# Cross attention turned in 32x32 blocks by VectorE and exchanged through DRAM

## The reference, cut to what matters

```python
q = (hidden_states @ Wq.T).reshape(bsz, q_len, H, HD).transpose(0, 2, 1, 3)
k = (cross_attention_states @ Wk.T).reshape(bsz, kv_len, KVH, HD).transpose(0, 2, 1, 3)
v = (cross_attention_states @ Wv.T).reshape(bsz, kv_len, KVH, HD).transpose(0, 2, 1, 3)
q = _rmsnorm(q, q_norm_w)
k = jnp.repeat(k, GROUPS, axis=1)
v = jnp.repeat(v, GROUPS, axis=1)
k = _rmsnorm(k, k_norm_w)
scores = jnp.einsum('bhqd,bhkd->bhqk', q, k) * scale
scores = scores + attention_mask[:, :, :, :kv_len]
probs = jax.nn.softmax(scores.astype(jnp.float32), axis=-1).astype(q.dtype)
out = jnp.einsum('bhqk,bhkd->bhqd', probs, v)
return out @ Wo.T
```

## Time and profile before

| | |
|---|---|
| Median of 3 runs | 789.96 us (789.69 to 791.82) |
| Profiled execution | 791.35 us |
| Span, first to last instruction | 789.6 us |
| Mean granted TensorE clock | 0.998 of 2.4 GHz |
| TensorE busy | 773.5 us (98%) |
| TensorE weight loads | 635.0 us (80%) |
| VectorE, ScalarE, POOL busy | 559.5 (71%), 414.7 (53%), 365.8 us (46%) |
| Moved by DMA | 34.63 MB |

### The profile page before, as it was taken

One profiled execution on the slowest core, in us unless ns is written; L12 is line 12 of the kernel. 1 busy time (PEld: TensorE's weight loads), 2 busy tenths in 40 slices (PEclk: granted clock), 3 DMA queues, 4 the chain that ended last, 5 costly groups with the idle time before them and its releaser, 6 DMA issues.

```text
span 789.6 us, 13246 instructions
## 1 busy us (share of the span) xinstructions
PE 773.5 (98%) x4260; PEld 635.0 (80%) x4260; DVE 559.5 (71%) x1235; ACT 414.7 (53%) x1158; POOL 365.8 (46%) x429
## 2 busy tenths in 40 slices
PE   8899999989999999999999999999999999999998
PEld 5555665778888888888888888888888888788776
DVE  5888886667766766777777776676677777667874
ACT  5566654565456545654655555555555654355421
POOL 1668856564246324632553364336433533254532
PEclk9999999999999999999999999999999999999999
DMA  8311012021003100300031012002100201000011
GB/s 295 129 41 41 15 50 98 1 94 29 14 1 107 28 1 1 108 28 1 3 107 27 1 32 87 18 1 73 49 14 1 81 1 54 1 15 1 1 40 68
DMA packets 17124, 34.63 MB, mean 44 GB/s; under 512 B 2336, under 2 KB 2592, under 8 KB 16800
## 3 DMA queue, kind: packets, MB, share of 16 engines
q1 hardware_dynamic: 17056, 33.78, 13.5%
HBM read 31.67 MB, written 2.10 MB: 43 GB/s over the span
## 4 chain that ended last, share of the span: by engine, by line
PE 77%; DVE 8%; POOL 7%; issue 5%; ACT 1%; DMA 1%; SPq 0%; POOLq 0%; DVEq 0%; ACTq 0%
PE pair L862 18%; PE pair L863 18%; PE pair L864 18%; PE pair L964 4%; PE pair L977 3%; PE pair L1026 3%; PE pair L902 3%; POOL qkr L526 2%; PE pair L876 2%; POOL probn L518 2%; PE pair L966 1%; POOL wo_lo L512 1%; DVE xres L1325 1%; DVE score L1342 1%; PE pair L919 1%
## 5 line engine op out<-in xcount | busy, mean ns | idle before, releaser
L518 POOL TENSOR_TENSOR probn<-prob,erec 128x512 f32<-128x512 f32 x64 | 66.8, 1044 | 169.5 <-DVE erec L1357 169.5
L1381 DVE TENSOR_TENSOR qkn<-pair,qkr 128x640 f32<-128x640 f32 x64 | 52.8, 824 | 91.6 <-POOL qkr L526 91.6
L1362 DVE TENSOR_REDUCE qkss<-qksq 128x5 f32<-128x640 f32 x64 | 52.6, 821 | 84.4 <-ACT qksq L720 84.4
L713 ACT ACTIVATE prob<-score,nmax 128x128 f32<-128x128 f32 x256 | 99.6, 393 | 21.0 <-DVE nmax L1344 19.2
L702 ACT ACTIVATE oT_hi<-pair 128x512 fp32r<-128x512 f32 x64 | 38.1, 595 | 136.2 <-PE pair L864 136.2
L862 PE MATMUL pair<-wq_hi,nT_hi 128*128 128x512 f32 x256 | 106.6, 416 | 0.0
L862 PE MATMUL pair<-wo_hi,oT_hi 128*128 128x512 f32 x256 | 100.9, 394 | 2.8 <-issue 2.8
L864 PE MATMUL pair<-wq_hi,nT_lo 128*128 128x512 f32 x256 | 101.0, 394 | 0.0
L863 PE MATMUL pair<-wq_lo,nT_hi 128*128 128x512 f32 x256 | 100.9, 394 | 0.0
L863 PE MATMUL pair<-wo_lo,oT_hi 128*128 128x512 f32 x256 | 100.4, 392 | 0.0
L864 PE MATMUL pair<-wo_hi,oT_lo 128*128 128x512 f32 x256 | 99.8, 390 | 0.0
(11 more groups left out here) (178 smaller groups left out, 1985.0 us busy)
## 6 DMA issues: line engine op xcount, KB each, us to landing
wq_raw<-in_wq SPq DMA_DIRECT2D x32, 256.0 KB, 3.1
wo_raw<-in_wo SPq DMA_DIRECT2D x32, 256.0 KB, 2.9
wkv_raw<-in_wkv SPq DMA_DIRECT2D x8, 512.0 KB, 4.8
ctxn<-in_ctx_n SPq DMA_DIRECT2D x8, 256.0 KB, 3.6
ctxt<-in_ctx_t SPq DMA_DIRECT2D x8, 256.0 KB, 2.7
out<-wkv_raw SPq DMA_DIRECT2D x8, 256.0 KB, 2.0
xres<-in_x SPq DMA_DIRECT2D x1, 1280.0 KB, 8.3
wbase<-in_wbase SPq DMA_DIRECT2D x1, 1024.0 KB, 7.5
```

Of the source, the lines that this page charges most:

```text
L518: pool.tensor_tensor(probn[:], prob[:], erec[:].unsqueeze(2).broadcast_to([P, HG, P]), ALU.mult).then_inc(normed, 1)
L713: t = act.activation(prob[:, h, :], score[:, h, :], ACT.Exp, bias=nmax[:, h:h + 1], accum_out=esum[:, h:h + 1])
L1362: dve.tensor_reduce(qkss[:], qksq[:], AX.X, ALU.add).then_inc(qk_ss, 1)
L1381: dve.tensor_tensor(qkn[:], qk_bank, qkr[:].unsqueeze(2).broadcast_to([P, HG + 1, P]), ALU.mult).then_inc(qk_nat, 1)
```

## The change

Queries, keys and probabilities are no longer turned by TensorE. VectorE's transpose turns each 32x32 block of the tile where it lies (`turn_qk`, `turn_probs` on VectorE); then the blocks must change places between the four quarters of the partitions. SP does this through DRAM (`write_blocks`): four writes, one for each 32 partitions, in runs of 640 bytes (queries and keys) or 512 bytes (probabilities), then one read with 128 rows of 2560 or 2048 bytes. DRAM has two such places for each kind. The turned queries lie as four blocks of 32 rows of all four heads, so the scores of block i hold rows 32 i to 32 i + 31 of the four heads; mask, maxima, sums and probabilities follow that order.

The scores are four plain fp32 matmuls of 128 columns; the high and low parts of queries and keys are gone, and `scale_keys` on ScalarE writes the scaled keys once. The mask is loaded ready in the new order, into the place of four of the `dft` matrices, and added in one VectorE instruction. The normalised probabilities are written in place. The freed PSUM banks give the scores one bank, the projections two pairs in turn from unit 3 on (`buf`).

Every `slot` has a new order. On TensorE: probabilities times values of n - 3, projections of n + 2, scores of n, output projection of n - 3; the way from scores to values is one unit longer. In the last slots `feed_forward` stands ahead of `turn_batch`. The output weights are split at unit 3 of a group instead of 1. SP's loop runs over the units: it writes and reads the blocks, and the weight loads stand at fixed units behind them.

The diff, cut to its core:

```diff
+    WKV_AT, WO_AT = 0, 3
+    WQ_AT = {1: (0,), 2: (1,), 4: (2,), 5: (3,)}
...
+        def buf(n):
+
+            return 1 + (n % 2 if n >= 3 else 0)
...
+                def write_blocks(n, tile, dram, turned, read, done):
+
+                    sp.wait_ge(turned, n + 1)
+                    if n >= 2:
+                        sp.wait_ge(read[n % 2], landed(n - 2))
+                    q = P // BL
+                    for i in range(BL):
+                        sp.dma_start(dram[n % 2][:, :, i, :].rearrange("j z r -> z j r"),
+                                     tile[i * q:(i + 1) * q, :].rearrange("z (j r) -> z j r", j=BL)).then_inc(
+                                         done[n % 2], 16)
...
+                def read_qk(n):
+                    sp.wait_ge(qk_out[n % 2], BL * landed(n))
+                    need(sp, s_done, n - 1)
+                    sp.dma_start(qkT[n % 2][:].rearrange("p i h y -> p (i h y)"),
+                                 qk_dram[n % 2].rearrange("j z i r -> (j z) (i r)")).then_inc(qk_in[n % 2], 16)
+
+                def read_probs(n):
+                    sp.wait_ge(p_out[n % 2], BL * landed(n))
+                    need(sp, p_h, n)
+                    need(sp, p_l, n)
+                    sp.dma_start(pTf[:], p_dram[n % 2].rearrange("j z h r -> (j z) (h r)")).then_inc(p_in[n % 2], 16)
...
+                for n in range(-1, N + 1):
+                    g, b = n // B, n % B
+                    if on(n + 1):
+                        write_qk(n + 1)
+                    if n < 2 and on(n + 1):
+                        read_qk(n + 1)
+                    if on(n - 1):
+                        write_probs(n - 1)
+                    if n >= 2 and on(n + 1):
+                        read_qk(n + 1)
+                    if on(n - 1):
+                        read_probs(n - 1)
...
                 def scores(n):
...
-                    for h in range(HG):
-                        w = slice(h * P, (h + 1) * P)
-                        pe.matmul(s_bank[:, h, :, :].rearrange("p i t -> p (i t)"), qT_hi[:, w],
-                                  kT[:].rearrange("p i t -> p (i t)"), start=True, stop=True, skip_group_check=True)
-                        t = pe.matmul(s_bank[:, h, 0, :], qT_lo[:, w], kT[:, 0, :], start=False, stop=True,
+                    for i in range(BL):
+                        t = pe.matmul(s_bank[:, i, :], queries(n, i), kT[:], start=True, stop=True,
                                       skip_group_check=True)
...
                 def slot(n):
-                    late = n % B == 2
-                    if on(n):
-                        scores(n)
-                    if on(n - 1):
-                        turn_probs(n - 1)
+                    if on(n - 3):
+                        probs_v(n - 3)
...
+                    if on(n + 2):
+                        project_qkv(n + 2)
+                    if batch(n, FEED) is not None:
+                        feed_forward(batch(n, FEED))
+                    if batch(n, TURN) is not None:
+                        turn_batch(batch(n, TURN))
+                    if on(n):
+                        scores(n)
...
+                    if on(n - 3):
+                        project_out(n - 3)
...
+                def turn_probs(n):
+                    need(dve, normed, n + 1)
+                    if n > 0:
+                        dve.wait_ge(p_out[(n - 1) % 2], BL * landed(n - 1))
+                    dve.transpose(p_blocks[:].rearrange("p (j i y) -> p i j y", j=BL, i=BL),
+                                  prob[:].rearrange("p i (j z) -> p i j z", j=BL)).then_inc(p_turned, 1)
...
+                def turn_qk(n):
+                    need(dve, qk_nat, n + 1)
+                    if n > 0:
+                        dve.wait_ge(qk_out[(n - 1) % 2], BL * landed(n - 1))
+                    dve.transpose(qk_blocks[:].rearrange("p (j h y) -> p h j y", j=BL, h=HG + 1),
+                                  qkn[:].rearrange("p h (j z) -> p h j z", j=BL)).then_inc(qk_turned, 1)
```

413 lines of the change are left out of this document (197 added, 216 removed).

## The result

The changed kernel takes 739.92 us (median of 4 runs, 738.72 to 740.52), the kernel before 790.86 (4 runs, 789.69 to 791.82). The ratio is 0.9355, with a 95% interval from 0.9334 to 0.9375: 51 us faster. The forecast was 732.5 in a range of 722 to 766, so it was 7.4 us low. The profiled execution took 738.72 us.

The account below looks back on a forecast made before the run. The prediction took TensorE, 98% busy, as the bound. The profiled 791.35 us, less 62 for 64 units, plus 1.4 (start) and 3.2 (end), gave 734.0; less 1.4 for the median, 732.6, forecast as 732.5, range 722 to 766.

Parts of the forecast that it names:

- Scores at the correlation's price, 0.90 us: TensorE, each unit: four fp32 score matmuls at the correlation's 0.224 us each, 0.90 us against 0.87 before.
- 1.8 us of slack: VectorE, each unit: 6.7 us of work in a unit of 8.5 us, so 1.8 us stay free.
- X: Probabilities' exchange through DRAM, four writes, landing, then read: 6.4 us, or 8.2 with weight loads between; hidden.
- 7.4 + X: Probabilities' loop through exchange, ScalarE and VectorE: least time for two units, 13.8 to 15.6 us against TensorE's 17.0.
- Rival B: Exchange becomes the bound, still faster: 9.0 us a unit, 764 us; 780 if writes land one by one. Chance 0.10.
- POOL's subtractions at unit 3 cost nothing: Output weights' split, four 1.30 us subtractions: VectorE's query scaling some 1.2 us late, but TensorE does not wait.
- Without the second bank it would be that 1.2 us eight times: Projections without alternating PSUM bank pairs: TensorE would wait for VectorE's late query scaling, 1.2 us eight times.
- The start, +1.4 us: First probabilities pass through DRAM: TensorE stands still 3.2 us; 4.2 us of waiting against 2.8 before, so +1.4.
- The end, +3.2 us: Last slots: turns of batches 6 and 7 exposed directly ahead of their matmuls, 1.6 us twice.
- A: The forecast itself: TensorE stays the bound at 8.5 us a unit, own range 722 to 745 us. Chance 0.76.
- C: VectorE's two turns at four cycles an element make VectorE the bound: 10.2 us a unit, 841 us. Chance 0.10.
- D: fp32 scores cost 1.84 us a unit and cancel the saved transposes: 792 us, no change. Chance 0.04.

Follow-up runs that it names:

- e1: Changed kernel with nine unread transposes per unit put back on TensorE in units 4 to 55; 789.62 us, ratio 0.9983 to the kernel before.
- e2: Kernel before with only the scores changed to four fp32 matmuls, transposes left on TensorE; 787.37 us, ratio 0.9965.
- e4: Changed kernel with both VectorE turns done twice in each unit, 774.82 us; a version with three times took 853.35 us.
- e5: Changed kernel without its DRAM exchange: VectorE turns straight into the readers' tiles, blocks left in wrong places; 733.64 us, ratio 0.9281.
- e3: Changed kernel reading the probabilities twice from DRAM, one read after the other has landed; 825.13 us, ratio 1.0435.
- e6: Changed kernel with all projections in one pair of PSUM banks instead of two in turn; 784.01 us, ratio 0.9922.
- e7: Changed kernel with ScalarE scaling each unit's keys at the start of their own slot, also in the last slots; 736.40 us, ratio 0.9313.
- e8: Changed kernel with the next batch's turn ahead of the current products in the last slots, ScalarE's high part ahead of exponentials; 735.79 us, ratio 0.9306.

## Why the prediction was right, and where it was off

**Transposes removed, 1.00 us a unit: right.** 9.49 - 8.47 = 1.02 us in an ordinary unit, both in the change and, the other way, in e1. With the interval of 9.00 behind unit 3 of each group the mean unit is 8.53 us against the forecast 8.51.

**Scores at the correlation's price, 0.90 us: right.** The forecast had them 0.03 us a unit dearer than before; in e2 the unit is 9.49 us with either form, so they cost nothing. The 0.81 us in the changed unit are no cheaper price: there a 512-column matmul follows them and no transpose, and its start is counted from another place.

**VectorE 6.7 us of 8.5: right; "1.8 us of slack": right in five units of eight only.** The turns came at 0.85 and 0.71 us for the assumed 0.82 and 0.69. By the Trainium skill, "Vector Engine (DVE) Microarchitecture Reference", section 3.8, the turn sustains one element per cycle per lane; the trace agrees in so far as 128 elements more take 0.13 us in the turn and 0.15 in plain operations (0.825 against 0.677). The share was an average over units with different loads: behind units 1 to 3 of a group e4 loses 1.1 to 1.8 us each.

**The exchange, X of 6.4 to 8.2 us, hidden with cover: right in size, 6.6 us in an ordinary unit, and right that it is hidden** (e5: 6.3 us in all, and no difference from unit 6 to unit 55). The loop "7.4 + X" for two units was drawn too small, since it left out ScalarE's and POOL's splits behind the landing. SP's own round of one unit was not worked out at all, although the round of 9.3 us in e3 shows that it can bind.

**A small packet's price, about 5 us of DMA in a unit: right, slightly dear.** (0.63 - 0.13) x 8.47 = 4.2 us by the windows of the changed kernel and e5. Had each of the four writes landed before the next one started (Rival B's tail), X would be 11.1 us; the trace has 6.6, with the writes issued 0.45 us apart and each landing 1.8 us after issue. The rule in the Trainium skill, "DMA: Bandwidth & Descriptors", rules for kernel authors, speaks of two halves that share the same 16 engines; these writes do not wait for each other's landing.

**"POOL's subtractions at unit 3 cost nothing": wrong by some 3 us.** I had thought of who waits for VectorE's scaling; what waits is the output projection, for the subtractions themselves. The page puts down 1.2 us, six waits of 0.2, but the interval behind unit 3 is 0.54 us longer in each of six groups, 3.2 us. **"Without the second bank it would be that 1.2 us eight times": right in its place, and only a part.** The interval behind unit 2 grows by 1.8 us in e6, and every ordinary one by 0.39; in all it is 44 us. I had named one late arrival that the banks hide, and missed the one in each unit.

**The start, +1.4 us: too small.** The wait for the first probabilities was forecast at 3.2 us and is 2.08, partly by luck: TensorE asks for them at 164.25, where the forecast had 161.9, and they are ready at 166.3 for 165.1. The wait for unit 1's bank was put at 1.0 and is 1.31. Two more before the scores of units 2 and 3 (1.04 and 1.38 us) and 0.94 in two small ones were not foreseen. From 130 to 206 us TensorE is idle 6.75 us against 2.98 in the same stretch before: +3.8.

**The end, +3.2 us: the named part was right, the list was incomplete.** The naked turns of the last two batches cost 1.75 + 1.46 = 3.21 us. "Elsewhere stalls of today's kind stay" is what failed here: the early keys on ScalarE (L817) bring 3.23 and 1.62 us at batches 0 and 1, and a second stretch at 1.2 GHz. From 640 us on TensorE is idle 9.05 us against 4.31 before: +4.7. e7 and e8 take these out.

**The sum.** TensorE's busy time fell by 61.4 us where 62 was forecast; idle time rose by 8.7 where 4.6 was. Start, middle and end account for it: 3.8 + 1.2 + 4.7, less 1.0 in the unchanged first layer. (The busy time hides 2 of the 3.2 us behind unit 3, and the ordinary units, at 8.47 for 8.51 us, give about as much back.) On the profiled execution the forecast was thus 734.0 against 738.72. The rest of the 7.4 us is how an execution stands to the median: I took off 1.4 us, and here the median is 1.2 above the profiled one. The lower end of A's own range, 722, is also 3 us too low by its own terms: 732.6 less 4.6 for start and end and 64 x 0.05 for the transposes is 724.8.

**The rivals.** B did not come: no engine or queue takes 9 us in a unit. C did not come, but was nearer than I worked out. D did not: the scores' form changes no unit (e2).

## What to carry to other kernels

Work taken from the engine that bounds the kernel comes back in full only where every loop that was hidden before stays shorter than the new, shorter unit. Price each loop by its waits in order, and by the busiest kind of unit, not by an engine's mean share: a wait on an in-order queue (SP for a landing, ScalarE for an exchange) passes to all that stands behind it. Measure a unit from start to start; busy time hid most of a wait here. And when a stage gets a new order, read the first and the last slots one by one; here they held another 8.9 us beside the 51.

## What the runs showed of the hardware

**VectorE's turn of 32x32 blocks of fp32 runs at its ordinary pace**: 845 ns for 128x640 and 711 ns for 128x512, though it reads and writes with a stride, against 825 and 677 for plain operations of these sizes (L1434, L1414).

**Smaller packets cost less, but not in proportion.** A packet of the changed kernel takes 0.526 x 16 x 736.9 / 109216 = 56.8 ns, at 1.0 KB in the mean, against 100 ns at 2.0 KB before. The 92160 that the change added take 49 ns each at 0.82 KB, an estimate from the difference of the two runs' queue rows.

**VectorE and POOL hold each other up when both read two SBUF operands.** POOL's subtraction `wo_lo` takes 1391 ns in the mean and 1743 at most, against 1295 and 1312 before; `wq_lo` 1387 against 1300. The subtraction for `pT_lo` takes 669 ns at least and 681 in the median, but up to 1749. VectorE, then POOL in the same stretch of the changed kernel:

```profile
361.36 1.53 DVE L1403 TENSOR_TENSOR pT_lo<-pTf,pT_hi 128x512 fp32r<-128x512 f32 x1
```

```profile
361.04 1.31 POOL L596 TENSOR_TENSOR wq_lo<-wq_raw,wq_hi 128x512 fp32r<-128x512 f32 x1 [0.52 <-ACT wq_hi L782]
```

VectorE's instruction starts at 361.36 and ends at 362.89; counted back by its 0.68 us, it got going at 362.21, about when POOL's was done (362.35). The other way round a unit later: VectorE's started first, and POOL's at 369.95 took 1.70 us (in the chain above) for its usual 1.30:

```profile
369.82 0.67 DVE L1403 TENSOR_TENSOR pT_lo<-pTf,pT_hi 128x512 fp32r<-128x512 f32 x1
```

Over 64 units that is (0.875 - 0.681) x 64 = 12 us on VectorE, and `oT_lo`, which reads one operand from PSUM, stays at 677 ns in the mean, though it runs beside POOL's product of the probabilities (359.95 beside 359.48 to 360.52). The Trainium skill, "SBUF — State Buffer", section "Who interferes with whom", says that the two share a pair of ports, that a VectorE instruction with two SBUF inputs contends with a POOL instruction that reads SBUF and one with at most one SBUF input does not, and that the one which starts first keeps the pair; this trace agrees on all three. Before the change the probabilities' low part read PSUM and had no such wait. On VectorE it costs no time in the units at 8.47 us. On POOL it may: in the four groups that I looked at, one of the four `wo_lo` subtractions takes 1.74 us instead of 1.30, and TensorE waits for the end of the last. By that 0.44 of the 0.54 us behind unit 3 would be this contention, an estimate that no run tested. The prediction should have counted it.
